# Scan of a state space layer: a quarter of the products with B goes over rows of tokens on ScalarE and TensorE, and the weights of the expert layer's inner norm are applied after the turn

## What is computed

```
dt = softplus(dt_low @ dt_proj + bias);  A = -exp(A_log)
h[t] = exp(dt*A) * h[t-1] + (dt * x) * B[t]      # for 256 channels x 16 states
y[t] = sum over states of h[t] * C[t]  + x*D

h1 = combine(dispatch(x) @ W1 + b1)              # 512 wide, by group of tokens
r  = relu(layer_norm(h1, eps=1e-6) * ln_w + ln_b)
out = combine(dispatch(r) @ W2 + b2)
```

## Time and profile before

| | us |
|---|---|
| median of 3 runs | 1603.75 (1603.72 to 1604.36) |
| the profiled execution | 1601.89 |
| its span, first to last instruction | 1600.1 |
| first and last scan instruction start (L643) | 123.6 and 844.1 |
| granted TensorE clock, mean | 0.912 |
| attention and second expert layer, last stretch | 1060 to 1600 |

### The profile page before, as it was taken

How to read it: one execution, slowest core, us unless ns; L and a number is a source line. 1 busy time by engine, 2 the same in 40 slices (tenths; PEclk the granted TensorE clock), 3 DMA queues, 4 the chain that set the end, 5 groups by cost and what they waited for, 6 DMA issues and landing times. The chain is left out here.

```text
span 1600.1 us, 21773 instructions
## 1 busy us (share of the span) xinstructions
PE 1342.1 (84%) x7560; PEld 918.6 (57%) x7560; DVE 1259.3 (79%) x2322; ACT 824.1 (52%) x1936; POOL 636.9 (40%) x592
## 2 busy tenths in 40 slices
PE   7968787879878757899885795379999999999998
PEld 5534344434333336788875573246677777777776
DVE  6669999998899899999995745828988655577667
ACT  5366565655656654566451454563454444444453
POOL 0036544325887745455423652009800212176000
PEclk9979999978887857999996698599999999999999
DMA  6014454543433213445424110200001133123001
GB/s 211 0 29 111 129 145 125 145 114 111 130 117 109 86 58 111 131 130 148 130 78 154 48 27 7 89 20 1 1 1 53 41 93 83 52 53 43 10 14 41
DMA packets 75891, 127.31 MB, mean 80 GB/s; under 512 B 11758, under 2 KB 38606, under 8 KB 75174
## 3 DMA queue, kind: packets, MB, share of 16 engines
q1 hardware_dynamic: 56326, 75.04, 15.6%
q0 software_dynamic: 19456, 50.88, 12.1%
HBM read 85.51 MB, written 40.37 MB: 79 GB/s over the span
## 5 line engine op out<-in xcount | busy, mean ns | idle before, releaser
L643 DVE TENSOR_TENSOR_SCAN sc_st<-sc_dA,sc_st 128x1024 f32<-128x1024 f32 x128 | 296.4, 2357 | 0.0
L2014 DVE COPY at_pT<-at_p_t 128x512 f32<-128x512 f32 (+1 forms) x192 | 109.4, 599 | 131.9 <-PE at_p_t L1907 131.8
L1965 ACT ACTIVATE at_pr<-at_p_s,at_nmx 128x512 f32<-128x512 f32 (+3 forms) x256 | 131.3, 527 | 130.7 <-DVE at_nmx L1991 130.6
L1191 POOL DMA_INDIRECT g_state<-xn_scratch,moe_tab x96 | 116.6, 1215 | 181.4 <-POOLq L99 101.7
L613 DVE TENSOR_TENSOR sc_st<-sc_u,sc_p_b 128x1024 f32<-128x1024 f32 x128 | 155.1, 1211 | 37.5 <-PE sc_p_b L483 21.6
L422 ACT ACTIVATE sc_dA<-sc_dt,g_state 128x511 f32<-128x511 f32 x256 | 169.2, 710 | 19.8 <-DVE sc_st L643 16.4
L1886 PE MATMUL at_p_s<-att_xaT,at_qT 128*128 128x512 f32 (+3 forms) x512 | 171.9, 458 | 0.0
L1920 PEld LDWEIGHTS at_p_o<-at_V,at_pT 128*128 128x128 f32 x1280 | 152.4, 192 | 29.6 <-issue 28.8
L1222 POOL DMA_INDIRECT g_state<-r_scratch,moe_tab x96 | 114.2, 1190 | 117.4 <-PE e_bank L1321 80.8
L621 DVE TENSOR_TENSOR sc_st<-sc_st,sc_p_c 128x1024 f32<-128x1024 f32 x128 | 155.2, 1213 | 0.0
L1920 PE MATMUL at_p_o<-at_V,at_pT 128*128 128x128 f32 x1280 | 153.7, 275 | 1.8 <-DVE g_state L2004 1.8
(11 more groups left out here) (295 smaller groups left out, 2753.8 us busy)
## 6 DMA issues: line engine op xcount, KB each, us to landing
y_scratch<-g_state SPq DMA_DIRECT2D x24, 768.0 KB, 5.3
g_state<-W SPq DMA_DIRECT2D x48, 256.0 KB, 5.2
r_scratch<-g_state SPq DMA_DIRECT2D x16, 512.0 KB, 2.7
y_scratch<-g_state SPq DMA_DIRECT2D x24, 192.0 KB, 2.9
xn_scratch<-g_state SPq DMA_DIRECT2D x16, 256.0 KB, 4.1
g_state<-x SPq DMA_DIRECT2D x4, 512.0 KB, 6.8
g_state<-xn_scratch SPq DMA_DIRECT2D x8, 256.0 KB, 6.1
g_state<-x SPq DMA_DIRECT2D x1, 2048.0 KB, 12.1
```

What stands on the lines that cost most here:

```text
L643: nc.vector.tensor_tensor_scan(st[:, m % RS, :, :].rearrange("p a b -> p (a b)"), dA[:, m % 4, :, :].rearrange("p a b -> p (a b)"), st[:, ...
L1191: nc.gpsimd.indirect_dma_start(out=self.xg[:, e % 4, h, :], out_offset=None, in_=self.xn_rows, in_offset=bass.IndirectOffsetOnAxis(ap=r.ta ...
L1965: ins = nc.scalar.activation(pr[:, n % 2, bank, c:c + K], p_s[:, bank, c:c + K], ACT.Exp, bias=nmx[:, n % 2, i:i + 1], accum_out=sums[:, n ...
L2014: v.tensor_copy(pT[:, n % 2, part, 0:cols], p_t[:, PT_BANK[part], 0:cols]).then_inc(pT_ready, 1)
```

## The change

1. In odd steps, times_b(i,1) and `broadcast_b(i,1)` go (32 of the 128 products with B). In their place ScalarE multiplies rows of tokens: once for each sequence TensorE turns `u` so that tokens are on partitions (`turn_u`, 8 transposes, copied to `uT` by ScalarE in two pieces) and picks the four rows of B that are needed as columns (`turn_b`, `copy_bT`). For each odd step, ScalarE makes `uB = uT * B` with the column of B as the scale (`scale_uT`, four Copy activations of 128x256), TensorE turns it back in two halves of four transposes (`turn_uB`) and ScalarE copies each half (128x512) from PSUM into `sc_st` (`copy_uB`), from which the scans read it.
2. All of this uses the PSUM bank `sc_p_b`, which before held only the broadcast B. In an even step i the two halves of `turn_uB(i+1)` go through it in turn, each copied out before the next, and `broadcast_b(i+1, 0)` waits for the second copy (`uB_copied`).
3. GpSimd's two products by `ln_w` and `ln_b` and ScalarE's Relu on the rows go. The rows are stored once they are centred. The weights are now one number for each partition after the turn: the copy of each item of the second layer (one Copy of 128x384) becomes four Relu activations of 128x96 with scale and bias from a tile. `ln_w` and `ln_b` are loaded as 128x16 instead of being spread over all partitions.
4. The nine weights of the output stage are loaded during the scan, after the first three loads of W2.

The core of the diff:

```diff
+        uT = s.sb("uT", [P, TB, DI])
+        uB = s.sb("uB", [P, TB, DI])
+        BT = s.sb("BT", [P, 2, TB, PAIRS // 2])
...
+        def by_rows(i):
+            return i % 2 == 1
+        def products(i, j):
+            return 2 * i + j - i // 2
...
+            def copy_uT(b, half):
+                act.wait_ge(u_turned, 2 * b + half + 1)
+                if b:
+                    act.wait_ge(uB_ready, PAIRS // 2 * b)
+                source = p_b[:, :] if b else p_c[:, half, :]
+                nc.scalar.activation(uT[:, 2 * half:2 * half + 2, :].rearrange("p t c -> p (t c)"), source,
+                                     ACT.Copy).then_inc(uT_ready, 1)
+            def scale_uT(i):
+                b, q = divmod(i, PAIRS)
+                act.wait_ge(uT_ready, 2 * b + 2)
+                act.wait_ge(bT_ready, b + 1)
+                if i > 1:
+                    act.wait_ge(uB_turned, 2 * (i // 2))
+                for t in range(TB):
+                    ins = nc.scalar.activation(uB[:, t, :], uT[:, t, :], ACT.Copy,
+                                               scale=BT[:, b % 2, t, q // 2:q // 2 + 1])
+                ins.then_inc(uB_ready, 1)
+            def copy_uB(i, h):
+                m = 2 * i + h
+                act.wait_ge(uB_turned, 2 * (i // 2) + h + 1)
+                if m >= RS:
+                    act.wait_ge(hc_used, m - RS + 1)
+                nc.scalar.activation(st[:, m % RS, 1, :], p_b[:, :], ACT.Copy).then_inc(uB_copied, 1)
...
+            copy_bT(0)
             decays(0, 0)
             decays(0, 1)
+            copy_uT(0, 0)
+            copy_uT(0, 1)
+            scale_uT(1)
             copy_dt_rank(1)
             for i in range(STEPS):
                 b, q = divmod(i, PAIRS)
...
                 if b + 1 < B and q == 1:
                     copy_mid(b + 1)
                 yield
+                if i + 1 < STEPS and by_rows(i + 1):
+                    copy_uB(i + 1, 0)
+                    copy_uB(i + 1, 1)
+                if q == 5 and b + 1 < B:
+                    copy_bT(b + 1)
+                if q == 7 and b + 1 < B:
+                    copy_uT(b + 1, 0)
+                    copy_uT(b + 1, 1)
                 if i + 1 < STEPS:
                     decays(i + 1, 1)
+                if i + 2 < STEPS and by_rows(i + 2):
+                    scale_uT(i + 2)
...
+                if by_rows(i):
+                    pe.wait_ge(uB_copied, 2 * (i // 2) + 2)
+                elif q == 0 and i:
+                    pe.wait_ge(uT_ready, 2 * b + 2)
+                elif q == 6 and b + 1 < B:
+                    pe.wait_ge(bT_ready, b + 2)
...
+            def turn_u(b, half):
+                pe.wait_ge(u_ready, 2 * b + 2)
+                if b and half:
+                    pe.wait_ge(uT_ready, 2 * b + 1)
+                elif b:
+                    pe.wait_ge(b_used, products(PAIRS * b - 1, 1))
+                out = p_b[:, :] if b else p_c[:, half, :]
+                for k in range(2):
+                    t = 2 * half + k
+                    for h in range(HALF):
+                        ins = nc.tensor.transpose(out[:, k * DI + h * P:k * DI + (h + 1) * P],
+                                                  u[:, b % 2, h, t * P:(t + 1) * P], w["ident"])
+                ins.then_inc(u_turned, 1)
+            def turn_uB(i, h):
+                if h:
+                    pe.wait_ge(uB_copied, 2 * (i // 2) + 1)
+                else:
+                    pe.wait_ge(uB_ready, i // 2 + 1)
+                    pe.wait_ge(b_used, products(i - 1, 1) + 1)
+                for t in range(TB):
+                    ins = nc.tensor.transpose(p_b[:, t * P:(t + 1) * P], uB[:, t, h * P:(h + 1) * P], w["ident"])
+                ins.then_inc(uB_turned, 1)
...
+            turn_b(0)
             broadcast_b(0, 0)
+            pe.wait_ge(bT_ready, 1)
+            turn_u(0, 0)
+            turn_u(0, 1)
             for i in range(STEPS):
                 b, q = divmod(i, PAIRS)
-                broadcast_b(i, 1)
+                if not by_rows(i):
+                    broadcast_b(i, 1)
                 if b + 1 < B:
                     if q == 1:
                         dt_project(b + 1, 0)
...
                 if b + 2 < B and q == 7:
                     x_project(b + 2)
                 yield
-                if i + 1 < STEPS:
+                if q == 5 and b + 1 < B:
+                    turn_b(b + 1)
+                if q == 7 and b + 1 < B:
+                    turn_u(b + 1, 0)
+                elif i + 1 < STEPS and not by_rows(i + 1) and q != 5:
                     broadcast_b(i + 1, 0)
                 if i:
                     sum_states(i - 1, 0)
                 broadcast_c(i)
+                if i + 1 < STEPS and by_rows(i + 1):
+                    turn_uB(i + 1, 0)
                 yield
+                if q == 7 and b + 1 < B:
+                    turn_u(b + 1, 1)
+                if q == 5:
+                    broadcast_b(i + 1, 0)
                 if i:
                     sum_states(i - 1, 1)
+                if i + 1 < STEPS and by_rows(i + 1):
+                    turn_uB(i + 1, 1)
                 yield
+                if i + 1 < STEPS and (by_rows(i + 1) or q == 7):
+                    broadcast_b(i + 1, 0)
...
-                times_b(i, 1)
+                if not by_rows(i):
+                    times_b(i, 1)
                 if i:
                     times_c(i - 1, 1)
                 yield
-                dve.wait_ge(b_used, 2 * i + 2)
+                dve.wait_ge(b_used, products(i, 0 if by_rows(i) else 1) + 1)
                 for h in range(HALF):
                     m = 2 * i + h
+                    if by_rows(i):
+                        dve.wait_ge(uB_copied, 2 * (i // 2) + h + 1)
...
+        for dst, src in self.next_weights:
+            sp.dma_start(dst, src).then_inc(self.next_in, 16)
         for u in range(self.UNITS):
             t = u * self.TILES
-            sp.wait_ge(self.r_ready, u + 1)
+            sp.wait_ge(self.centred, t + 2)
...
-        def weigh(u):
-            pool.wait_ge(self.centred, 2 * u + 2)
-            t = 2 * u
-            ro = self.ro[:, t % 6:t % 6 + 2, :]
-            g = slice(t % HG, t % HG + 2)
-            nc.gpsimd.tensor_tensor(ro, ro, self.w["ln_w"][:, g, :], ALU.mult).then_inc(self.p_chain, 1)
-            pool.wait_ge(self.p_chain, u + 1)
-            nc.gpsimd.tensor_tensor(ro, ro, self.w["ln_b"][:, g, :], ALU.add).then_inc(self.weighted, 1)
...
-            if 4 <= u:
-                n = u - 4
-                act.wait_ge(self.weighted, n + 1)
-                rows = ro[:, 2 * n % 6:2 * n % 6 + 2, :]
-                nc.scalar.activation(rows, rows, ACT.Relu).then_inc(self.r_ready, 1)
...
-                nc.scalar.activation(self.rT[:, n % 3, :], bank[:, 0, 0:FC * CP], ACT.Copy).then_inc(self.rT_ready, 1)
+                for f in range(FC):
+                    ins = nc.scalar.activation(self.rT[:, n % 3, f * CP:(f + 1) * CP], bank[:, 0, f * CP:(f + 1) * CP],
+                                               ACT.Relu, scale=self.w["ln_w"][:, h, f:f + 1],
+                                               bias=self.w["ln_b"][:, h, f:f + 1])
+                ins.then_inc(self.rT_ready, 1)
...
-        for dst, src in self.weights:
-            sp.dma_start(dst, src).then_inc(self.weights_in, 16)
...
-        "ln_w": c(i["L0_ffn_ln_hid_w"][None]),
-        "ln_b": c(i["L0_ffn_ln_hid_b"][None]),
+        "ln_w": c(i["L0_ffn_ln_hid_w"].reshape(HG, FC, P).transpose(2, 0, 1)),
+        "ln_b": c(i["L0_ffn_ln_hid_b"].reshape(HG, FC, P).transpose(2, 0, 1)),
```

51 lines of the change are left out of this document (38 added, 13 removed).

## The result

The changed kernel takes 1697.25 us (median of four runs, 1690.73 to 1699.44) where the kernel before took 1604.05: a ratio of 1.0574 with a 95% interval of 1.0544 to 1.0603. It is slower, as forecast, but by 93 us where 44 were forecast, and outside the range of 1608 to 1685. The profiled execution has a span of 1694.8 us, 94.7 more than before.

A forecast was written before the change was run, and what follows sets the result against it. VectorE was taken to bound the scan, some 730 of 1600 us. The terms -18 + 68 - 2 + 2 - 2 - 4 gave +44 on 1601.9, so 1645.9, and 1648 as median; range 1608 to 1685.

The forecast's parts named there:

- GpSimd, what goes: Combining: 17 to 18 us of VectorE's time blocked by GpSimd goes; counted -18 us, bounds -24 and -6.
- ScalarE, what comes: ScalarE's item copies: four activations take 1.52 us for 0.487, +99 us in all, plus scalings and copies for the rows.
- Rival C: Second layer: four short activations cost little, below 1.09 us, VectorE stays the bound; -40 us, 1564 us, chance 0.07.
- The second layer: Experts' second layer: the bound moves to ScalarE, 258 us busy plus 28 of waits, 286; +68 us, bounds +41 and +90.
- the wait of 28: Second layer: ScalarE's idle time, from hand-overs between item copies (18), the second `copy_uB` (7) and adjoining places (3).
- The bank in the other stretches: Outside the second layer: VectorE waits 1.1 us for the bank, about what the removed product saved; -2 us, bounds -13 and +23.
- Rival E: The bank's chain costs 3 us per pair of steps: +23 in the first stretch, combining's gain shrinks; +84, 1688 us, chance 0.12.
- rival D: Second layer: TensorE's clock falls as it waits for ScalarE, stretch about 325 us at 60%; 1687 us, chance 0.08.
- D's own condition: Second layer: TensorE's 198 us of work passes 286 if half the time is spent at the lower clock.
- A: The forecast itself: ScalarE, with its waits, bounds the second layer; 1648 us, own range 1627 to 1674, chance 0.55.
- The ends: Start of the scan +2 us, odd steps beside no experts -2, output stage -4 from earlier loads of `xn`.
- The 36 us of products: Scan: 32 products with B removed from VectorE free 1.11 us each, 36 us if nothing takes their place.

The follow-up runs named there:

- e14b: The changed kernel once more, unchanged, on another chip beside the kernel before: ratio 1.0563.
- The fold alone: Kernel before with the inner norm's weights and Relu moved from the rows into the item, both products with B left on VectorE: ratio 1.0046 with early loads.
- e2: Kernel before with four Relus per item, no GpSimd products and early output-weight loads; both products with B stay on VectorE: 1610.87 us, ratio 1.0046.
- e4: Kernel before without GpSimd's products, with one Relu of 384 columns per item (weights left out) and early output-weight loads: 1576.77 us, ratio 0.9835.
- e15: e4's kernel with ScalarE's part of the rows added on a constant, into a tile that nothing reads: ratio 0.9959.
- e5: Changed kernel with the product for an odd step's first product with B issued ahead of the expert layer's piece: ratio 1.0556.
- e13b: Changed kernel with one transpose in place of four per half of the bank (three quarters of odd steps' products left out): ratio 1.0470.
- e12b: Changed kernel with the first product of every second-layer item made three times, the first two overwritten, to fill TensorE: ratio 1.0563.
- e8: Kernel before with the inner norm's Relu made in the item's one copy and GpSimd's products cut into halves of 128x512: ratio 0.9992.
- e11: Kernel before with odd norm groups weighted by four Relus per item, even groups on GpSimd, output weights loaded early, no rows for the scan: ratio 1.0039.
- e9: e2's kernel with two Relus of 192 columns per item instead of four of 96, weights of every second block left out: ratio 0.9911.

## Why the prediction was wrong

The direction was right and the mechanism half right. By its own steps:

- **GpSimd, what goes** (-18): right in kind, and to the microsecond by luck. The combining is 18.2 shorter, but 27.1 in e14b. The fold alone gives 25 (e2, e4), since VectorE was blocked for 24.0 us and not for the 17 to 18 that I had added up from scans and L1440, and the rows take back up to 7. No scan is over 2337 ns, and the two-column operation answering to L1440 in the earlier trace rows has a mean of 160 ns.
- **ScalarE, what comes** (an item of 1.52 us, bounds 0.7 and 1.64): nearly right. Four Relus take 1.40 us (756.64 and 766.09 in the trace), 134.2 us for 96 items, +87 instead of +99. The estimate from the Trainium skill (ScalarE: Activation LUTs, What ACT_TABLE_LOAD costs), 1.53, was as close as the one from the nearest row, 1.52: both are 0.12 to 0.13 too high. Rival C, which needed 1.09 or less, is out.
- **The second layer: the step that failed.** I wrote that ScalarE would be busy for 258 us and wait for 28, "so +68". The stretch grew by 92.5. Its busy time was sized well enough: it grew by 116 us, to 244.9, where I had 133. The term that failed is the wait of 28: ScalarE is idle for 75.0. (My 217.3 us were one step shorter than the 227.3 here.) So it is busy for 77% and not over 85%, and VectorE waits not for decays or copies, as I had it, but for its product with B. The idle time was built from one hand-over at TensorE's full clock, transposes right behind a copy, as in the earlier trace rows. I had TensorE at hand for all of them, and it was not: it stands in its queue at one item's transposes while the scan's products wait behind them, it has 13 us more to do for the rows, and behind waits like the one at 765 us it works at the lower clock. e4 and e2 show that even without rows a circle of waits, not ScalarE's sum, sets the price of the Relus: 0.39 us for each us from the first one on, while ScalarE is busy for 57% (e4) to 82% (e2). My arithmetic, "no loss up to the length of the stretch, then all", with the 21 us of waits that do not come from the rows, would have given e2 213 + 21 = 234 us, a loss of 7; it has 33.
- **The bank in the other stretches** (-2, bounds -13 and +23): failed too, near its upper bound. +22.4 in the first layer (+19.3 in e14b). I had followed one step at a time with ScalarE free. e15 shows that 11 of 22 us come with no bank at all, from ScalarE's later copies for the experts' pieces; the rest comes through the chain and TensorE, and how it divides between these two was not separated (the profiled executions of e5 and e13b gave none of it back).
- **Rival E** had this right (+23) but gave the combining back wrongly and left the second layer at +68; **rival D** had the fall of TensorE's clock and asked for half of the time at the lower level. It falls to 0.87 over the stretch, and e12b puts 15 us of TensorE's busy time or more on that, no new bound. (D's own condition was worked out wrongly: with 1.91 us against 1.03, 198 us of work of which half the time runs at the lower level take 257, not 286; it needed two thirds of the time.) What happened is parts of A, D and E at once: I had given each a chance as if they shut each other out, and the range ended at each one's price, not at their sum.
- **The ends.** Start +0.6 for +2. In the output stage TensorE no longer waits for weights; the changed kernel there, to stand beside the earlier trace rows:

```profile
952.38 3.67 SPq L1605 DMA_DIRECT2D g_state<-xn_scratch  x8
...
952.41 3.44 PE L856 MATMUL mo_p_o<-moe_out_T,mamba_xT 128*128 128x128 f32 x16 [0.94 <-PEq L317]
...
955.99 0.69 DVE L959 TENSOR_TENSOR mo_z<-mo_p_o,g_state 128x512 f32<-128x512 f32 x1 [3.49 <-PE mo_p_o L856]
```

VectorE's first addition comes 3.6 us after the loads of `xn` begin, where before it came 7.4 after them, and it waits 3.49 us for it instead of 11.36. From step 63 on to this addition 8 us were won, yet the end came only 2.4 sooner: the rest was given back later in the stage, which I did not follow.

## What to carry to other kernels

Work moved from a full engine to one with room is not free up to that engine's capacity. Here three engines hand pieces round through one buffer in fixed queues, and each microsecond added to ScalarE was on the path in part long before it was full (0.24 to 0.40 of it alone, 0.77 for the Relus once the rows were there: 66.1 us for 85.9). Price it by the queues behind each waiting instruction, and look at the loads together, for two changes that cost 33 and 26 to 32 alone cost 92 together. The 36 us of products that VectorE was spared gained nothing beside the experts, as it waited for the bank instead. Taking away GpSimd's products, which made VectorE's operations longer, gained at once, and what replaced them cost more (33 us for 25).

## What the runs showed of the hardware

- Short waits of TensorE can cost twice: behind 3.19 us of waiting it ran eight matmuls in 1.92 us instead of 1.04, at a granted clock of 0.50. Over a stretch with 69 us of idle time in 320 its granted clock was 0.87, with 23 of 227 it was 0.95. The share of idle time alone does not tell, though: e2 had 46 of 261 at 0.95, and e14b's first layer 55 of 262 at 0.96. With 63.9 us of matmuls added whose results are thrown away the clock was 0.93 and the stretch only 5 to 10 us longer.
- GpSimd's two-input products of 128x1024 beside VectorE's scans cost the stretch 25 us for 85.8 us of GpSimd's work (e2, e4). VectorE's operations there were longer by 24.0 us in sum, the scans by 10.5 of it. Pieces of half the length cost the same (e8), and with half of the products about 20 us of the 25 stayed (e11).
- A Relu of 96 columns out of the bank with scale and bias from a tile takes 433 ns, four in a row 1.40 us. With 192 columns for each pair of pointers (e9) one takes 507 ns, and an item's ScalarE time fell by 0.46 us.
